# Values' bias moved from TensorE to VectorE, second-layer weights prepared in smaller pieces, and a reordered start, in a two-layer conditioned attention kernel

## The reference

```python
# layer 0: full attention
xn = layer_norm(x, norm_w, norm_b)
q = (xn @ q_w + q_b); k = (xn @ k_w + k_b)                 # reshaped to 16 heads
att = softmax(q @ k.T + (1 - mask) * -1e6, axis=keys)
v = (xn @ v_w + v_b) * mask
y = att @ v
scale, shift = split(silu(cond) @ emb_w + emb_b)
h = layer_norm(y, sb_norm_w, sb_norm_b) * (1 + scale) + shift
x = x + silu(h) @ out_w + out_b
# layer 1: linear attention
xn = layernorm(x); q, k, v = xn @ Wq + bq, xn @ Wk + bk, xn @ Wv + bv
k = where(mask_i == 1, -inf, k); v = where(mask_i == 1, 0, v)
q = softmax(q, head dim); k = softmax(k, sequence)
y = q @ (k.T @ v)                                           # by head
... same scale/shift, silu, output product and residual as layer 0
```

## Time and profile before

| | us |
|---|---|
| median of 3 runs | 976.47 (976.24 to 977.93) |
| the profiled execution | 977.76 |
| its span, first to last instruction | 976.0 |
| TensorE matmuls busy | 916.1 (94%) |
| VectorE busy | 772.6 (79%) |
| ScalarE busy | 709.6 (73%) |
| GpSimd busy | 581.9 (60%) |

### The profile page before, as it was taken

The page is one execution under the profiler, slowest core; times in us unless marked ns, Lnnn a source line. Parts: engine busy times, 40 slices in busy tenths (PEclk is TensorE's granted clock), DMA queues, the critical chain, the costliest instruction groups (busy, mean ns, idle before and its releaser), DMA issues.

```text
span 976.0 us, 24849 instructions
## 1 busy us (share of the span) xinstructions
PE 916.1 (94%) x8880; PEld 760.1 (78%) x8880; DVE 772.6 (79%) x1536; ACT 709.6 (73%) x1328; POOL 581.9 (60%) x1033
## 2 busy tenths in 40 slices
PE   5789999999999999999999767999999999999996
PEld 4666767777777777777776436999999999999995
DVE  5568988888888888888887733888888888888874
ACT  2257677777777777777777665788888888888874
POOL 3343636454545555555554224688888888888874
PEclk9999999999999999999999978999999999999998
DMA  8733333334343434343424112212233222223101
GB/s 263 242 113 116 136 137 136 138 123 150 115 158 118 154 115 159 112 156 115 158 103 147 67 60 86 68 45 77 77 91 99 78 76 77 77 86 97 43 29 54
DMA packets 77402, 108.62 MB, mean 111 GB/s; under 512 B 7072, under 2 KB 43392, under 8 KB 77152
## 3 DMA queue, kind: packets, MB, share of 16 engines
q1 hardware_dynamic: 77280, 107.03, 32.6%
HBM read 35.60 MB, written 16.88 MB: 54 GB/s over the span
## 4 chain that ended last, share of the span: by engine, by line
PE 82%; DVE 8%; issue 6%; POOL 2%; ACT 1%; SPq 0%; DMA 0%; POOLq 0%; DVEq 0%; ACTq 0%
PE psX L1041 14%; PE psY L1141 13%; PE psM L1041 10%; PE psT L1041 9%; PE psM L1120 8%; PE psT L1105 7%; PE psY L1041 4%; PE psT L1289 3%; PE psT L1052 3%; PE psM L1052 3%; PE psY L1258 3%; DVE sb_cm L808 3%; PE psY L1160 2%; DVE sb_yr L825 2%; PE psX L1052 1%
## 5 line engine op out<-in xcount | busy, mean ns | idle before, releaser
L808 DVE TENSOR_REDUCE sb_cm<-psM 128x4 f32<-128x1024 f32 x256 | 313.3, 1224 | 86.6 <-PE psM L1120 77.8
L516 ACT ACTIVATE sb_P<-psT 128x1024 f32<-128x1024 f32 x256 | 262.1, 1025 | 16.9 <-PE psT L1105 13.6
L1141 PE MATMUL psY<-sb_P,sb_Vp 128*17 128x256 f32 x2048 | 137.9, 387 | 8.9 <-DVE sb_yr L825 8.3
L372 POOL TENSOR_SCALAR sb_ve<-sb_mv 128x2 f32<-128x2 f32 x32 | 7.1, 221 | 230.8 <-DVE sb_mv L833 230.8
L1120 PE MATMUL psM<-sb_Ks,sb_Qs 64*128 64x256 f32 x1024 | 118.5, 309 | 11.8 <-DVE sb_cm L808 11.6
L1105 PEld LDWEIGHTS psT<-sb_Qs,sb_Ks 64*128 64x128 f32 x1024 | 78.2, 188 | 60.2 <-issue 53.8
L1105 PE MATMUL psT<-sb_Qs,sb_Ks 64*128 64x256 f32 x1024 | 120.0, 313 | 0.0
L530 ACT ACTIVATE sb_qp<-psX,sb_bq 128x256 f32<-128x256 f32 x122 | 51.2, 471 | 74.8 <-PE psX L1041 74.8
L1120 PEld LDWEIGHTS psM<-sb_Ks,sb_Qs 64*128 64x128 f32 x1024 | 77.5, 186 | 32.9 <-DVE sb_cm L808 17.3
L1041 PE MATMUL psX<-sb_xT,sb_W0h 128*128 128x256 f32 x488 | 95.3, 298 | 1.9 <-DVE sb_xT L815 1.1
L1141 PEld LDWEIGHTS psY<-sb_P,sb_Vp 128*17 128x17 f32 x2048 | 49.4, 97 | 53.3 <-issue 15.6
(11 more groups left out here) (179 smaller groups left out, 2445.2 us busy)
## 6 DMA issues: line engine op xcount, KB each, us to landing
sb_Qs<-sb_qp SPq DMA_DIRECT2D x96, 256.0 KB
sb_Ks<-sb_qp SPq DMA_DIRECT2D x96, 256.0 KB
sb_xt<-in_x SPq DMA_DIRECT2D x32, 256.0 KB, 3.1
y_normed<-sb_Yn SPq DMA_DIRECT2D x32, 256.0 KB, 2.0
sb_u<-in_x SPq DMA_DIRECT2D x32, 256.0 KB, 2.9
sb_u<-y_normed SPq DMA_DIRECT2D x32, 256.0 KB, 3.1
out<-sb_w SPq DMA_DIRECT2D x32, 256.0 KB, 2.2
sb_v<-key_mask SPq DMA_DIRECT2D x32, 128.0 KB, 3.5
```

The lines of the kernel that those rows point to most:

```text
L516: a.activation(P[G % 4][:, :], psT[G % 2][:, :], ACT.Exp).then_inc(s_ex, 1)
L808: v.tensor_reduce(cm[n % 2][:, 4 * j:4 * j + 4], psMM[:, :].rearrange("p (k t) -> p k t", k=4), AX.X, ALU.max, negate=True).then_inc(s_mx, 1)
L1141: ins = pe.matmul(psY[32 * j:32 * j + 17, 0:T], Vp[n % RING][:, m, 4 * gr + j, :], Pj[:, c0:c0 + 256], start=(m == 0), stop=(m == 1))
```

## The change

- Values' bias: `vals` loses the two bias matmuls and c64, vbx and their preparation go. VectorE's new `vbias` (step 7, behind reduce) adds the bias while it copies the values from psX to the new tile vb; GpSimd's new `vmask` (step 7, behind xnorm) scales vb by the mask into Vp. xturn and three other waits of TensorE now wait for vbias (s_vb).
- Second layer: film, the W1 weights and the output weights become 28 pieces (`for_later`), one behind the work of each of steps 2, 4 and 6 from turn 5 to turn 14.
- Front: ScalarE's queue issues the three weight loads of the first layer; the identity, the bias row and the fill pattern's copy have semaphores of their own; the columns are loaded earlier; GpSimd makes the mask parts; VectorE normalizes sequence 0 behind the q weights and splits the v weights before it normalizes sequence 1; the masks are transposed on TensorE at step 5 of turn 0 and copied by ScalarE at step 6.

```diff
-LOADS = (4, 2, 1, 5)
+LOADS = (3, 1, 1, 5)
...
+            sp.dma_start(ident[:, :], ident_d).then_inc(s_id, 16)
+            sp.dma_start(col[:, :, :], cols).then_inc(s_ld[1], 16)
             sp.dma_start(mrow[:, :], mask_f).then_inc(s_ld[0], 16)
             sp.dma_start(irow[:, :], mask_i).then_inc(s_ld[0], 16)
             sp.dma_start(fr[:, :, :], fill).then_inc(s_ld[0], 16)
-            sp.dma_start(col[:, :, :], cols).then_inc(s_ld[1], 16)
-            for n in range(2):
-                sp.dma_start(W0[:, n, :, :], weights[:, 0, n]).then_inc(s_lw[n], 16)
             xload(1)
-            sp.dma_start(W0[:, 2, :, :], weights[:, 0, 2]).then_inc(s_lw[2], 16)
-            sp.dma_start(rb[:, 0, :], rows[0:1, :].to_broadcast([128, D])).then_inc(s_ld[1], 16)
+            sp.dma_start(rb[:, 0, :], rows[0:1, :].to_broadcast([128, D])).then_inc(s_rb, 16)
             sp.dma_start(cond_sb[:, :], cond).then_inc(s_cond, 16)
+            sp.wait_ge(p_ones, 1)
+            filled(0)
+            sp.wait_ge(s_lw[2], 16)
             sp.wait_ge(p_ve, 4)
             sp.dma_start(md.rearrange("b c t -> b (c t)"), mp[:, :, :]).then_inc(s_md, 16)
-            sp.wait_ge(p_act, 1)
-            filled(0)
-            sp.wait_ge(s_lw[2], 16)
             sp.dma_start(EW[:, :, :, :], emb).then_inc(s_ld[2], 16)
             sp.wait_ge(s_md, 16)
-            sp.wait_ge(p_pool, 3)
+            sp.wait_ge(p_pool, 2)
...
-            g.memset(c64[:, :], 1.0 / 64).then_inc(p_pool, 1)
...
-                if n == 1:
+                if n <= 1:
                     return
...
+            def vmask(n):
+                if n == 0:
+                    g.wait_ge(p_act, 3)
+                g.wait_ge(s_vb, n + 1)
+                if n >= RING:
+                    g.wait_ge(s_pv, 4 * (n - RING) + 4)
+                for k in range(2):
+                    ins = g.tensor_scalar(Vp[n % RING][:, k, :, 0:16], vb[:, k, :].rearrange("p (h d) -> p h d", d=DH),
+                                          mT[:, k, n:n + 1], 1.0, ALU.mult, ALU.mult)
+                ins.then_inc(s_v, 1)
+
+            g.wait_ge(p_pool, 2)
             xnorm(0)
+            g.wait_ge(s_ld[0], 16 * LOADS[0])
+            g.tensor_scalar(mr2[:, :], mrow[:, :], -1.0, 1.0, ALU.mult, ALU.add).then_inc(p_ve, 1)
+            g.wait_ge(p_ve, 1)
+            g.tensor_scalar(mr2[:, :], mr2[:, :], -1000000.0, 0.0, ALU.mult, ALU.add).then_inc(p_ve, 1)
+            g.wait_ge(p_ve, 2)
+            g.tensor_scalar(mp[:, 0, :].bitcast(F32R), mr2[:, :], 1.0, 0.0, ALU.mult, ALU.add).then_inc(p_ve, 1)
+            g.wait_ge(p_ve, 3)
+            g.tensor_tensor(mp[:, 1, :].bitcast(F32R), mr2[:, :], mp[:, 0, :], ALU.subtract).then_inc(p_ve, 1)
...
+                    if i == 7 and ok(t):
+                        vmask(t)
...
+            for n in range(3):
+                a.dma_start(W0[:, n, :, :], weights[:, 0, n]).then_inc(s_lw[n], 16)
             a.wait_ge(s_ld[0], 16 * LOADS[0])
-            a.activation(ones[:, :, :].bitcast(F32R), fr[:, :, :], ACT.Identity)
-            a.wait_ge(p_pe, 1)
-            for k, dst in enumerate((mT, kT)):
-                ins = a.activation(dst[:, :, :], psX[:, 2 * B * k:2 * B * k + 2 * B].rearrange("p (k b) -> p k b", k=2),
-                                   ACT.Identity)
-            ins.then_inc(p_act, 1)
-            a.wait_ge(p_act, 1)
+            a.activation(ones[:, :, :].bitcast(F32R), fr[:, :, :], ACT.Identity).then_inc(p_ones, 1)
...
-            def vmask(n):
-                a.wait_ge(s_vm, n + 1)
-                if n >= RING:
-                    a.wait_ge(s_pv, 4 * (n - RING) + 4)
-                for k in range(2):
-                    ins = a.activation(Vp[n % RING][:, k, :, 0:16],
-                                       home("v", n)[:, 256 * k:256 * k + 256].rearrange("p (h d) -> p h d", d=DH),
-                                       ACT.Identity, scale=mT[:, k, n:n + 1])
-                ins.then_inc(s_v, 1)
...
+                if (t, i) == (0, 6):
+                    a.wait_ge(p_pe, 3)
+                    for k, dst in enumerate((mT, kT)):
+                        ins = a.activation(dst[:, :, :], R[3][:, 2 * B * k:2 * B * k + 2 * B]
+                                           .rearrange("p (k b) -> p k b", k=2), ACT.Identity)
+                    ins.then_inc(p_act, 1)
...
+            def high(n):
+
+                v.wait_ge(s_lw[n], 16)
+                for k in range(2):
+                    ins = v.tensor_scalar(W0h[:, n, k, :].bitcast(F32R), W[0][n][:, k, :], col[:, 0, k:k + 1], None,
+                                          ALU.mult)
+                ins.then_inc(s_w0, 1)
+
+            def low(n):
+
+                v.wait_ge(s_w0, 2 * n + 1)
+                for k in range(2):
+                    ins = v.scalar_tensor_tensor(W0l[:, n, k, :].bitcast(F32R), W[0][n][:, k, :], col[:, 0, k:k + 1],
+                                                 W0h[:, n, k, :], ALU.mult, ALU.subtract)
+                ins.then_inc(s_w0, 1)
+
+            def first_norm(n):
+                v.wait_ge(s_rs, 3 * n + 3)
+                if n:
+                    v.wait_ge(s_xtr, n)
+                for k in range(2):
+                    ins = v.tensor_scalar(xn[:, k, :], xt[n][:, k, :], mv[:, k, 0:1], rs[:, k:k + 1], ALU.subtract,
+                                          ALU.mult)
+                ins.then_inc(s_xn, 1)
+
+            v.wait_ge(s_ld[1], 16 * LOADS[1])
+            high(0)
+            low(0)
+            first_norm(0)
...
+            def film(m):
+
+                if m < 2:
+                    v.wait_ge(p_act, 7)
+                    for d in range(2):
+                        v.tensor_scalar(sc[:, m, d, :], ev[:, m, d, :], col[:, m, 8 + d:9 + d], 1.0, ALU.add, ALU.add)\
+                            .then_inc(p_film, 1)
...
+            def second_weight(n, part, k):
...
+                    v.tensor_scalar(W1h[:, n, k, :].bitcast(F32R), W[1][n][:, k, :], col[:, 1, k:k + 1], None, ALU.mult)\
+                        .then_inc(s_w1, 1)
...
+                    v.wait_ge(s_w1, 4 * n + 2)
+                    v.scalar_tensor_tensor(W1l[:, n, k, :].bitcast(F32R), W[1][n][:, k, :], col[:, 1, k:k + 1],
+                                           W1h[:, n, k, :], ALU.mult, ALU.subtract).then_inc(s_w1, 1)
...
+                    v.wait_ge(s_wo, 3 * l + 1)
+                    v.tensor_tensor(Wol[l][:, m - 1, :].bitcast(F32R), Wo[l][:, m - 1, :], Woh[l][:, m - 1, :],
+                                    ALU.subtract).then_inc(s_wo, 1)
+
+            def for_later(m):
+
+                if m < 10:
+                    film(m)
+                elif m < 22:
+                    second_weight((m - 10) // 4, (m - 10) // 2 % 2, m % 2)
+                elif m < 28:
+                    out_weight((m - 22) // 3, (m - 22) % 3)
...
+            def vbias(n):
+
+                v.wait_ge(s_vm, n + 1)
+                if n == 0:
+                    v.wait_ge(p_vb, 1)
+                else:
+                    v.wait_ge(s_v, n)
+                v.tensor_tensor(vb[:, :, :], home("v", n).rearrange("p (k d) -> p k d", k=2),
+                                rb[:, 0:1, :].to_broadcast([128, 2, D]), ALU.add).then_inc(s_vb, 1)
...
                 if (t, i) == (0, 2):
                     v.wait_ge(p_pe, 4)
+                    v.wait_ge(s_rb, 16)
                     v.tensor_tensor(rb[:, 0, :], rb[:, 0, :], psY[:, 0:256], ALU.add).then_inc(p_vb, 1)
-                    v.wait_ge(p_vb, 1)
-                    v.tensor_copy(vbx[:, :].bitcast(F32R), rb[:, 0, :]).then_inc(p_vb, 1)
-                    v.wait_ge(p_vb, 2)
-                    v.tensor_tensor(vbx[64:128, :].bitcast(F32R), rb[64:128, 0, :], vbx[64:128, :], ALU.subtract)\
-                        .then_inc(p_vb, 1)
...
-                if t == 5 and i % 2 == 1:
-                    film(i // 2)
-                if t in (6, 7, 8) and i in (1, 5):
-                    scaled(1, t - 6, i // 4)
-                if t in (9, 10) and i in (1, 5):
-                    out_weight(t - 9, i // 4)
...
-                    first_weight(1)
+                    high(1)
+                    low(1)
+                    v.wait_ge(s_ld[0], 16 * LOADS[0])
+                    v.tensor_scalar(mr3[:, :], irow[:, :], 1, None, ALU.is_equal).then_inc(p_mneg, 1)
+                    v.wait_ge(p_mneg, 1)
+                    v.tensor_scalar(keep[:, :], mr3[:, :], -1.0, 1.0, ALU.mult, ALU.add).then_inc(p_mneg, 1)
+                    v.wait_ge(p_mneg, 2)
+                    v.tensor_scalar(mr3[:, :], mr3[:, :], NEG, None, ALU.mult).then_inc(p_mneg, 1)
                     stats(1, 0)
                     stats(1, 1)
-                    v.wait_ge(s_rs, 6)
-                    v.wait_ge(s_xtr, 1)
-                    for k in range(2):
-                        ins = v.tensor_scalar(xn[:, k, :], xt[1][:, k, :], mv[:, k, 0:1], rs[:, k:k + 1],
-                                              ALU.subtract, ALU.mult)
```

(34 more changed lines are left out.)

115 lines of the change are left out of this document (34 added, 81 removed).

## The result

| | us |
|---|---|
| before, median of 4 runs on the same chip | 976.36 (975.60 to 977.93) |
| after, median of 4 runs | 963.28 (961.19 to 965.66) |
| ratio | 0.9869 [0.9842, 0.9896] |
| the profiled execution of after | 961.19 |
| its span | 959.3 |

The forecast was 963.2 us and the median is 963.28. The number was met; the sum behind it wasn't, so that the agreement is luck. One of its three terms, the largest, is worth nothing that could be measured, another is worth nearly twice what it was put at, and only the third came out about as forecast. A forecast that is right for such a reason has to be taken apart like a wrong one.

A forecast was written before the change was run, and what follows sets the result against it. TensorE was taken to bound the kernel, holding 82% of the chain of waits. Gains of 5.0 (front), 4.7 (bias) and 3.6 (small steps) made 13.3 us: 964.5 for the profiled execution, 963.2 for the median, range 958.0 to 969.5.

The forecast's parts named there:

- Part 1: In each first-layer turn, two bias matmuls leave TensorE for vbias and GpSimd scaling: 4.7 us gained in all.
- I charge all 0.09: In a steady turn, xturn waits 0.09 us longer for vbias, and all of it reaches the q product.
- The gap of 0.21 us: TensorE's idle time before the attention-by-values product; as a bound, it swallows vbias's delay, leaving 0.24 us gain per turn.
- The 0.5 us for turns 1 to 3: Early turns of the first layer: 0.24 us gained each, less about 0.2 in all.
- Part 2: Turns 4 to 11: cutting the second layer's preparations into 28 pieces removes most of 4.40 us excess, gaining 3.6 us.
- the 0.8 us left for late pieces at step 6: Nine pieces at step 6 end late and delay TensorE through vbias, taking 0.8 us off the 4.4.
- The rule of the Trainium skill that spoke against it: VectorE and GpSimd instructions lock each other out; each small piece meeting GpSimd would cost 0.7 us more, not 0.1.
- Rival (d): Small steps gain nothing: excess is loop filling, or step 6 pieces meet GpSimd's normalization; 966.8 us, chance 0.08.
- Part 3: First 30 us: reordered loads and VectorE work start turn 1 earlier, gaining 5.0 us, bounds 3.5 and 6.5.
- The 1.7 us by which the first product was to be earlier: At the front, VectorE is free for xlow sooner, so TensorE's first product starts at about 10.2, not 11.9.
- rowmax(0) with no wait for a DMA: Sign at the front: sequence 0's first row-maximum product finds its k data landed, with 2 us to spare.
- first product of turn 1 at 21.3: Sign for the front: TensorE's first product of turn 1 starts at 21.3 us, where before had 26.33.

The follow-up runs named there:

- bias_alone: The kernel before with only the values' bias moved to VectorE, its scaling to GpSimd and its splitting gone: 968.58 us beside 977.37, ratio 0.9915.
- front_alone: The changed kernel with its bias move and small pieces undone, so only the front is new: 977.87 us beside 977.37 for before, ratio 1.0003.
- steps_alone: The kernel before with only the second layer's preparations cut into small pieces at steps 2, 4 and 6: 972.96 us, ratio 0.9958.
- after_again: The changed kernel run once more, unchanged, for a second trace: 963.99 us, ratio 0.9859 to before.
- no_front: The kernel before with the bias moved and the small pieces, without the new front: 964.58 us, ratio 0.9877.
- w0_sync: The changed kernel with only the three weight loads put back on SyncE's queue: 962.09 us, ratio 0.9838 to before.
- before_again: The kernel before run once more, unchanged, one execution for a second trace: span 973.4 us.
- best: Against w0_sync: sequence 0 normalized ahead of the low weights, table load cut in two, pieces at steps 2 and 4 only: 962.33 us, ratio 0.9852.

## Why the prediction was right, and where it wasn't

- **Part 1, put at 4.7, is 8 to 9.** The 0.24 us of two matmuls were right, and so were vbias's start (1.14 after the reduction) and its length (0.68). xturn's delay was twice what I had taken, 0.18 for 0.09, since the handover from vbias took the 0.14 that I had only as a bound. The step that failed is "I charge all 0.09": of the delay 0.05 was left at the value product and 0.03 at the q product, near the upper bound that I had named. The gap of 0.21 us that I had named for it did not close, as said above; the slack lay in the rows ahead of it. That gives 0.21 in 28 turns, 5.9 us for 4.2. The other 2 us lay ahead of turn 1. I had seen them (1.2 us "with a wait for the split bias and two slow bias matmuls") and booked them under the front; bias_alone has them without any reordering, front_alone doesn't have them. The 0.5 us for turns 1 to 3 can't be read: that stretch varies by more than 1 us between executions of one kernel (50.31 and 48.63 in the kernel before).
- **Part 2, put at 3.6, is about 4.** The mechanism held, and 3.6 lies inside the interval of steps_alone (2.4 to 5.7 us). Of the 0.8 us left for late pieces at step 6 nothing came, but 0.4 are left over turns 4 to 14 for another reason. The rule of the Trainium skill that spoke against it (SBUF — State Buffer, "Who interferes with whom", VectorE and GpSimd locking each other out) does show in after, at step 4, where GpSimd's subtraction runs; the same form of operation in two places of the loop, with GpSimd's of that time between them, and around them the marks of turns 9 and 10:

```profile
151.90 0.68 DVE L833 TENSOR_TENSOR sb_xT<-psX,sb_xT 128x512 fp32r<-128x512 f32 x1
...
154.41 0.45 DVE L802 SCALAR_TENSOR_TENSOR sb_W1l<-sb_W,sb_col,sb_W1h 128x256 fp32r<-128x256 f32 x1
...
157.90 1.29 POOL L384 TENSOR_TENSOR sb_qp<-sb_qp 128x512 fp32r<-128x512 f32 x1
...
158.46 1.02 DVE L802 SCALAR_TENSOR_TENSOR sb_W1l<-sb_W,sb_col,sb_W1h 128x256 fp32r<-128x256 f32 x1
...
168.18 0.68 DVE L833 TENSOR_TENSOR sb_xT<-psX,sb_xT 128x512 fp32r<-128x512 f32 x1
```

  The second piece ends 0.29 after GpSimd's 159.19, at 159.48: stretched by 0.57, near the 0.7 of the row. Most of that falls into idle time, but not all: this turn takes 16.28 us. Rival (d) named the right behaviour and the wrong place for it: at step 6 the pieces meet no such operation (0.32 us for a scaling at 146.62, 0.74 for the same at step 4 at 142.35). The three turns of after in which the piece at step 4 takes 1.02, 1.00 and 0.96 us last 16.28, 16.26 and 16.23, and those in which it takes 0.74 to 0.88 last 16.11 to 16.14, although all of them have a piece at step 6 too. The same three turns are the long ones in after_again, no_front, w0_sync and steps_alone. So what is left of the excess are the pieces at step 4 that GpSimd holds up for longest, 0.1 to 0.2 us each.
- **Part 3, put at 5.0, is 0 within 2 us.** The failed step is the base of the working. 2.78 us of its gain was a wait that a second execution of the same kernel had at 0.92, since it came from a chance meeting of two operations; 1.2 was part 1's. The 1.7 us by which the first product was to be earlier (10.2 for 11.9) were taken back by the loads: I had bounded x of sequence 0 at 1 us late, and it was 1.75 in after and 1.1 to 1.5 in the other three traces with the second queue (4.58 to 4.97 against 3.50); the first product stands at 11.73, and at 10.52 in w0_sync. The 0.92 went to TensorE's own list, to the mask transpositions that now stand in it and to a slow pace that lasted longer in this execution. The Trainium skill's rule (DMA: Bandwidth & Descriptors, "Queues, rings and completion order", each DMA engine takes turns between its queues) agrees in kind with the 3.50, 5.25 and 3.51 us of before_again, after and w0_sync; the delay of 1.75 us is more than the 1.0 us that I had worked out by it. And "rowmax(0) with no wait for a DMA", 2 us to spare, was wrong: 0.75 us of wait in after (none in after_again), 1.10 in best. The last part of k left SyncE at 22.10 and not at 18.9, and the table's load at 11.95 rather than 9.17; which of the two made the wait no run separates.
- **The sum.** -0.5 + 8.8 + 4.4 by the medians of single parts stands for 5.0 + 4.7 + 3.6. The errors, 5.5 us too much for one part and 4.9 too little for the two others, cancelled. Nothing in the working made them cancel. The case behind the figure (first product of turn 1 at 21.3) didn't occur: it was 22.92. Of the signs to watch, the turn of 16.18 was 16.12, the 1.9 us from reduction to xturn 1.96, turns 4 to 11 under 114.1 were 113.01.
- **Still open**: what the queue of the weights costs in time, the 0.6 us by which the whole change lies under no_front, and why the clock falls in one execution and not in the next.

## What to carry to other kernels

Before a gain is built on a wait of the first microseconds, look at a second execution of the same kernel: a wait that comes from two operations meeting by chance isn't there to be won, while the length of a steady turn agreed to 0.02 us here and can be trusted. An idle time in the rows can be free for other work even where it doesn't shrink: what counts is how late the next instruction starts. Move work to another engine into idle time behind the operation that must not be late, in pieces no longer than that idle time; place and size each gave less than half of what both gave. Look also at what runs on GpSimd at that moment, since a piece can take twice its time beside it. And when a start is reordered, price the loads that the new queue sets beside the one everybody waits for, and ask which DMA is late next. Before a lost gain is put down to the loads, look at the granted clock of the same stretch.
